# Repeated target rows merged over four tiles in place of two in the last eight batches of a two-layer graph kernel

## The reference, cut to what matters

```python
h = jnp.maximum(_layernorm(x, axis=-1), 0.0)
x_i, x_j = h[dst], h[src]
feat = jnp.concatenate([x_i, x_j - x_i], axis=-1)      # 512 per edge
msg = jax.nn.relu(feat @ W1 + b1) @ W2 + b2            # 512 -> 512 -> 256
out = segment_sum(msg, dst); deg = segment_sum(1, dst)
x = x + out / (deg + 1e-08)
```

## Time and profile before

| | |
|---|---|
| median of 3 runs | 2122.19 us (2121.31 to 2128.58) |
| profiled execution, its time | 2127.77 us |
| profiled execution, its span | 2125.6 us |
| granted TensorE clock, mean over the span | 0.912 |
| busy in the span: PE, DVE, POOL, ACT | 79%, 69%, 60%, 47% |

### The profile page before, as it was taken

One profiled execution on the slowest core, in us unless ns is written; L12 is line 12 of the kernel. 1 busy time (PEld: TensorE's weight loads), 2 busy tenths in 40 slices (PEclk: granted clock), 3 DMA queues, 4 the chain that ended last, 5 costly groups with the idle time before them and its releaser, 6 DMA issues.

```text
span 2125.6 us, 46204 instructions
## 1 busy us (share of the span) xinstructions
PE 1685.9 (79%) x13740; PEld 1478.3 (70%) x13740; DVE 1470.8 (69%) x5883; ACT 1006.6 (47%) x2064; POOL 1272.0 (60%) x1004
## 2 busy tenths in 40 slices
PE   4958788788855565650499999999999999999991
PEld 1237777678855554640389888888888888888881
DVE  6968898889965655640377777777766767777660
ACT  0014444445433232320366766667665656656561
POOL 2013333358878878875444333378888888888854
PEclk9979999999988787775699999999999999999996
DMA  7989999846665655654999999965555555555543
GB/s 242 317 290 322 323 324 332 276 101 109 111 103 91 98 94 97 98 72 72 333 328 330 336 331 331 335 143 97 95 93 92 98 91 98 92 92 97 93 65 39
DMA packets 140467, 376.43 MB, mean 177 GB/s; under 512 B 31391, under 2 KB 95656, under 8 KB 127528
## 3 DMA queue, kind: packets, MB, share of 16 engines
q0 software_dynamic: 84672, 128.51, 34.3%
q1 hardware_dynamic: 27452, 208.63, 27.6%
q10 hardware_dynamic: 28304, 38.85, 7.0%
HBM read 323.36 MB, written 258.12 MB: 274 GB/s over the span
## 4 chain that ended last, share of the span: by engine, by line
POOL 22%; DMA 13%; issue 12%; SPq 5%; ACT 0%; DVE 0%; POOLq 0%; ACTq 0%
POOL table_out L951 12%; DMA table_out<-x 11%; POOL ends L939 10%; SPq L926 5%; DMA table_out<-e_ring,e_targets_all 2%; ACT ends L1162 0%; DMA ends<-x,keys 0%; DVE e_moments L1013 0%; SPq L922 0%; ACT hid L1176 0%; DVE feat_lo L1080 0%; ACT feat_hi L1169 0%; ACT hid_hi L1179 0%; ACT e_ring L1194 0%; POOLq L949 0%
## 5 line engine op out<-in xcount | busy, mean ns | idle before, releaser
L939 POOL DMA_INDIRECT ends<-x,keys x392 | 398.9, 1018 | 309.5 <-PE ps_h L1263 107.4
L468 POOL DMA_INDIRECT x<-slots,targets_all x196 | 327.7, 1672 | 87.6 <-issue 56.4
L951 POOL DMA_INDIRECT table_out<-e_ring,e_targets_all x196 | 321.5, 1640 | 92.0 <-issue 55.8
L788 PE MATMUL ps_deg<-table,hot 128*128 128x128 bf16 x5488 | 329.5, 222 | 52.0 <-issue 26.5
L788 PEld LDWEIGHTS ps_deg<-table,hot 128*128 128x128 bf16 x5488 | 315.9, 99 | 61.5 <-issue 48.6
L453 POOL DMA_INDIRECT slots<-in_x,row_idx x196 | 210.2, 1072 | 239.7 <-DMA slots<-in_x,row_idx 170.2
L802 PE MATMUL ps_sum<-msg_hi,same 128*128 128x260 f32 x784 | 158.7, 334 | 207.1 <-issue 200.4
L1263 PE MATMUL ps_h<-feat_hi,w_hi 128*128 128x512 f32 x784 | 314.5, 401 | 10.4 <-DVE feat_lo L1080 5.3
L1263 PE MATMUL ps_h<-feat_lo,w_hi 128*128 128x512 f32 x784 | 310.3, 396 | 0.0
L1263 PE MATMUL ps_h<-feat_hi,w_lo 128*128 128x512 f32 x784 | 310.3, 396 | 0.0
L802 PEld LDWEIGHTS ps_sum<-msg_hi,same 128*128 128x128 f32 x784 | 135.2, 237 | 213.2 <-issue 213.2
(11 more groups left out here) (141 smaller groups left out, 3420.4 us busy)
## 6 DMA issues: line engine op xcount, KB each, us to landing
table_out<-x SPq DMA_DIRECT2D x400, 252.0 KB
x<-in_x SPq DMA_DIRECT2D x400, 250.0 KB
hi_row<-hi_rows ACTq DMA_DIRECT2D x49, 256.0 KB
src_row<-src_rows ACTq DMA_DIRECT2D x49, 256.0 KB
dst_row<-dst_rows ACTq DMA_DIRECT2D x49, 256.0 KB
ends<-x,keys POOLq DMA_INDIRECT x392
slots<-in_x,row_idx POOLq DMA_INDIRECT x196
x<-slots,targets_all POOLq DMA_INDIRECT x196
```

The lines of the kernel that those rows point to most:

```text
L468: pool.indirect_dma_start(out=x1_d, out_offset=bass.IndirectOffsetOnAxis(ap=targets_all[:, b, j:j + 1], axis=0), in_=slots[:, b % SLOTS, j ...
L788: last = nc.tensor.matmul(ps_deg[q][k][:, j * P:(j + 1) * P], hot[:, c, k, j * P:(j + 1) * P], table[:, c, part, :], start=(c == 0 and par ...
L939: pool.indirect_dma_start(out=ends[b % NE][:, n, :], out_offset=None, in_=x1_d, in_offset=bass.IndirectOffsetOnAxis(ap=keys[:, 1 - end, at ...
L951: pool.indirect_dma_start(out=out, out_offset=bass.IndirectOffsetOnAxis(ap=e_targets_all[:, b, j:j + 1], axis=0), in_=e_ring[:, b % RING1, ...
```

## The change

From batch 41 (`TAIL`) to 48 the set in which repeated rows are merged is the whole batch of four tiles. `sums` then takes four products per output tile and part in place of two, `peers` and `peers_after` are 512 wide in place of 256, and `scatter_end` waits once per batch, behind the second group. The loop is shortened to batches 1 to 40, since the merge width is a constant of the code. For the room the ring shrinks from 20 batches to 17.

```diff
-    RING1 = 20
+    RING1 = 17
+    TAIL = 41
...
-            peers = [sb(f"peers{q}", [P, W, G * P], fp32r) for q in range(2)]
-            after = sb("after", [P, G, G * P], bf16)
-            peers_after = sb("peers_after", [P, W, G * P], bf16)
+            peers = [sb(f"peers{q}", [P, W, W * P], fp32r) for q in range(2)]
+            after = sb("after", [P, W, W * P], bf16)
+            peers_after = sb("peers_after", [P, W, W * P], bf16)
...
-            QUADS = (NB - 1) // NE - 1
+            QUADS = (TAIL - 1) // NE
+            def merged(b):
+                return W if isinstance(b, int) and b >= TAIL else G
...
-                    pool.wait_ge(e_scattered, 16 * G * (GROUPS * b + g + 1))
+                    if (g + 1) * G % merged(b) == 0:
+                        pool.wait_ge(e_scattered, 16 * G * (GROUPS * b + g + 1))
...
                 def sums(b, q):
                     pe.wait_ge(peers_ready, b + 1)
+                    M = merged(b)
                     for g in range(GROUPS):
-                        pe.wait_ge(out_lo_done, GROUPS * b + g + 1)
+                        pe.wait_ge(out_lo_done, GROUPS * b + (g + 1 if M == G else GROUPS))
                         pe.wait_ge(e_in_ring, GROUPS * b + g + 1)
-                        for a in range(G):
+                        for a in range(G * g, G * g + G):
+                            w = a // M * M
                             for n, part in enumerate((out_hi, out_lo)):
-                                for j in range(G * g, G * g + G):
-                                    last = nc.tensor.matmul(ps_s[g][:, a * D:(a + 1) * D],
-                                                            peers[q][:, j, a * P:(a + 1) * P], part[:, j, :],
+                                for j in range(w, w + M):
+                                    last = nc.tensor.matmul(ps_s[g][:, a % G * D:(a % G + 1) * D],
+                                                            peers[q][:, j, (a - w) * P:(a - w + 1) * P], part[:, j, :],
```

More of the change, by code:

```diff
@@ L1002, in _ @@
                 dve.wait_ge(after_made, 1)
-                nc.vector.memset(after[:, 0, P:G * P], 1.0)
-                nc.vector.tensor_copy(after[:, 0, 0:P], later[:])
-                nc.vector.tensor_copy(after[:, 1, P:G * P], later[:]).then_inc(after_made, 1)
+                for a in range(W):
+                    if a + 1 < W:
+                        nc.vector.memset(after[:, a, (a + 1) * P:W * P], 1.0)
+                    last = nc.vector.tensor_copy(after[:, a, a * P:(a + 1) * P], later[:])
+                last.then_inc(after_made, 1)
                 dve.wait_ge(after_made, 2)
@@ L1039, in peers_of @@
                     dve.wait_ge(e_summed, GROUPS * b)
+                    M = merged(b)
                     for j in range(W):
-                        g = j // G
-                        last = nc.vector.tensor_scalar(peers[q][:, j, :], dst_row[q][:, g * G * P:(g + 1) * G * P],
+                        w = j // M
+                        last = nc.vector.tensor_scalar(peers[q][:, j, 0:M * P], dst_row[q][:, w * M * P:(w + 1) * M * P],
                                                        dst_col[q][:, j:j + 1], None, ALU.is_equal)
@@ L1046, in after_of @@
                 def after_of(b, t, q, u, v):
+                    M = merged(b)
                     for j in range(W):
-                        g = j // G
+                        w = j // M
                         last = nc.vector.scalar_tensor_tensor(
-                            peers_after[:, j, :], dst_row[q][:, g * G * P:(g + 1) * G * P], dst_col[q][:, j:j + 1],
-                            after[:, j % G, :], ALU.is_equal, ALU.mult, accum_out=n_after[:, j:j + 1])
+                            peers_after[:, j, 0:M * P], dst_row[q][:, w * M * P:(w + 1) * M * P], dst_col[q][:, j:j + 1],
+                            after[:, j % M, 0:M * P], ALU.is_equal, ALU.mult, accum_out=n_after[:, j:j + 1])
                     last.then_inc(n_after_done, 1)
@@ L1282, in sums @@
                     pe.wait_ge(peers_ready, b + 1)
+                    M = merged(b)
                     for g in range(GROUPS):
-                        pe.wait_ge(out_lo_done, GROUPS * b + g + 1)
+                        pe.wait_ge(out_lo_done, GROUPS * b + (g + 1 if M == G else GROUPS))
                         pe.wait_ge(e_in_ring, GROUPS * b + g + 1)
-                        for a in range(G):
+                        for a in range(G * g, G * g + G):
+                            w = a // M * M
                             for n, part in enumerate((out_hi, out_lo)):
-                                for j in range(G * g, G * g + G):
-                                    last = nc.tensor.matmul(ps_s[g][:, a * D:(a + 1) * D],
-                                                            peers[q][:, j, a * P:(a + 1) * P], part[:, j, :],
-                                                            start=(n == 0 and j == G * g),
-                                                            stop=(n == 1 and j == G * g + G - 1))
+                                for j in range(w, w + M):
+                                    last = nc.tensor.matmul(ps_s[g][:, a % G * D:(a % G + 1) * D],
+                                                            peers[q][:, j, (a - w) * P:(a - w + 1) * P], part[:, j, :],
+                                                            start=(n == 0 and j == w),
+                                                            stop=(n == 1 and j == w + M - 1))
                         last.then_inc(e_summed, 1)
```

## The result

The changed kernel took 2109.5 us in the median (2107.2 to 2114.8, 5 runs), the kernel before 2122.2 (2119.8 to 2128.6, 5 runs): ratio 0.9938, 95% interval 0.9915 to 0.9962, 12.7 us less. A second set of runs of both on another occasion gave 0.9946 (0.9929 to 0.9964). All ratios here are to the kernel before, run beside the kernel in question.

A forecast was written before the change was run, and what follows sets the result against it. POOL's own chain of scatter and landing was taken to set the end. Removed landing waits gave 13.36 and 0.95 us, 14.3 in all, every other term 0: 2122.2 - 14.3 = 2107.9 us, range 2104.5 to 2110.5.

The forecast's parts named there:

- What bounds: At the end POOL is 29 us behind its supply, so its own chain of scatter and landing sets the end.
- The removed waits: Eight landing waits in batches 41 to 48: 0 at 41, 0.95 us at 42, 13.36 for six; 14.3 us.
- The wait behind four scatters: Behind g1 of each merged batch, unchanged, cost 0; rival that landing grows with four in flight: 2121.2 us, chance 0.04.
- PE: `sums` gets 32 products in place of 16: 1.90 us more a batch, costing the end nothing.
- The lag at `sums(48)`: PE's delay ahead of batch 48's `sums`: 1.5 + 3.8 = 5.3 us.
- the covers: Time from ring entry written to POOL wanting it: 3.5 us (batch 47's g1), 4.1 and 5.9 (batch 48's g0, g1).
- The case of a supply-bound end: Rival: PE can't use the slack in steps 42 to 46, lag 8.0 us more, time 2112.4; chance 0.20.
- DVE and POOL: Hold-up in the merged batches taken as none; rival: 18.2 us more on POOL's chain, time 2126.1; chance 0.04.
- my sign for this in the tail: `line 957` spans above 1.6 us in the tail would show DVE holding POOL up.
- The added DVE time: Wider `peers` and `peers_after`: at most 3.1 us a batch, or 2.3; cost 0.
- The ring: At 17 batches, batch 17 g0's write has 18.6 us of cover, cost 0; rival that it stalls ACT: chance 0.02.

The follow-up runs named there:

- ring 17: The kernel before with the ring cut from 20 batches to 17 and nothing else; ratio 1.0009 (0.9987 to 1.0031).
- the other gather pace: The changed kernel with 27 gathers to 10 groups in place of 11 to 4; ratio to before 0.9934 (0.9912 to 0.9956).

## Why the prediction was right

**Time.** 2107.9 was forecast, 2109.5 measured, inside the range; a gain of 14.3 against 12.7, whose interval (8 to 18 us) holds both.

**What bounds.** POOL's chain of scatters and landings set the end before, and sets it now. The tail with all waits kept (79.4) and with the waits removed (63.5) shows it by itself.

**The removed waits.** Six idle times of 2.44 to 2.68 us became 0.30, as summed. The tail shrank by 15.6 us, 1.3 more than the sum. The surplus has the size of one difference: ahead of g0 of batch 45 the profile before had an idle of 4.46 us, the one after 3.08. It was no accident of one profile: the four variants of the kernel before (ring 17, and the three with wide comparisons) had 3.45, 4.01, 4.24 and 4.22 us there, the changed kernel with its waits kept 3.10. What makes it long was not tried. The wait behind four scatters, taken as that behind two, is 3.02 to 3.17 us; layer 0's fours were the right witness that landing doesn't grow with the number in flight, and the low 2.4 us there only lacked what layer 1's step from batch to batch adds. The first scatters of batch 43 came 7.93 us behind the last gather, as 8.88 - 0.95 would have it. The six gave 13.4 us, as the rows had it. The estimate from the fixed 2.0 us a transfer of the Trainium skill (DMA: Bandwidth & Descriptors, "Anatomy of one DMA") was 12 us, 1.4 too low.

**PE.** Products went at 0.12 us, twice as many per batch. The lag at `sums(48)`, against the last gather, is (82.25 - 29.65) - (82.95 - 34.32) = 4.0 us, where I had 5.3: over-sized by 1.3. POOL also came 1.3 us earlier than forecast, so the covers, 3.7, 4.1 and 5.9, came out as predicted (3.5, 4.1, 5.9) by luck: two errors cancel. The case of a supply-bound end is refuted for this kernel and shown to be near: 3.7 us later it begins, as with the other gather pace.

**DVE and POOL: the one step that was mis-sized.** I set the hold-up of POOL by DVE at nothing, from scatters of 1.55 us beside `peers_after`, and noted that no row shown had a scatter beside `peers`. The trace of before had such scatters, that at 2024.46 among them. The runs show a small hold-up, 10.7 us for 28 batches or 0.38 us a batch with DVE wide everywhere, and 3.8 us for 16 batches with merging from batch 25; five or six merged batches in the stream then cost some 1.4 to 2 us. That is within the spread of the stream itself (641.0 and 641.4 with the change, 638.4 and 639.6 in two of its variants, 636.9 to 639.5 without), so it is worked out, not seen. It has about the size of the difference between the tail's gain (15.6) and the median's (12.7), which is no proof: the interval of the latter is 10 us wide. Spans of line 957 above 1.6 us, my sign for this in the tail, did appear (1.93 and 1.91), but the tail of before had 1.99, 1.69 and 1.90, so the sign tells nothing. The added DVE time itself was over-sized: four `peers` plus four `peers_after` grew by about 1.6 us, not 2.3 to 3.1. An instruction has a part that doesn't double with its width: `peers` went from 0.35 to 0.48 us, so 0.22 of the 0.35 are no matter of its 256 elements.

**The ring.** Free at 17, 0.64 us of wait at 16, as the cover of 18.6 us against 20.5 us a batch has it.

**What is open.** The medians of one kernel move by several us from occasion to occasion. In the profiles that lies ahead of the first scatter (1383 to 1396 us) and in the stream; why was not tried. No variant beats the changed kernel beyond the intervals; merging from batch 43 does the same with less work.

## What to carry to other kernels

A landing wait is worth removing only where nothing stands between the transfers and the wait: here six of eight, and a seventh, with one gather in front, was worth 0.95 us. Price it by its own idle time minus the plain distance between two instructions. Then lay the time at which each transfer's data is ready beside the time at which the shortened chain will ask for it; what is left between the two is all that a further step in the same direction can bring.

## What the runs showed of the hardware

POOL's indirect transfers take longer to issue beside DVE's comparisons: with both comparisons doubled in width in all batches, 26 ns more per gather and 27 ns per scatter in the mean, some 0.2 to 0.3 us of stream per us of added DVE work. Gathers beside `peers`, a tensor_scalar, went from 1.05 to 1.14 us when it alone was widened, and those beside `peers_after`, a scalar_tensor_tensor with a sum, from 1.08 to 1.17; beside neither they stayed at 1.00 to 1.01.

The Trainium skill (SBUF — State Buffer, "SBUF: two separate sides") tells of a lock that a VectorE tensor_scalar in a two-port mode takes and that keeps POOL from writing descriptors. The tensor_scalar here fits such a mode: its further 256 elements take 0.13 us, about two in a cycle by an estimate with that page's 0.96 GHz. The four `peers` were slower as well beside the slow scatters (1.28 to 1.47 us in place of 1.14), so each seems to hold the other up. But over the stream POOL loses only 0.2 to 0.3 of the added time, and the scalar_tensor_tensor, at 0.27 us for 256 elements, holds POOL up as well. Why it does in that second case these runs do not tell.
